# GpSimd layer norm in a fused cross-attention and FFN block: mean subtracted in the normalising instruction

## What is computed

```
def _layernorm(x, axis=-1, eps=1e-05):
    m = jnp.mean(x, axis=axis, keepdims=True)
    v = jnp.var(x, axis=axis, keepdims=True)
    return (x - m) / jnp.sqrt(v + eps)
...
    x = x + _L0_xattn_ref(_layernorm(x, axis=-1), ctx_1024, ctx_1024, mask_SxS2_bk1, ...)
    x = x + _L0_ffn_ref(_layernorm(x, axis=-1), L0_ffn_w1, L0_ffn_b1, L0_ffn_w2, L0_ffn_b2)
```

## Time and profile before

| | |
|---|---|
| median of 3 runs | 397.78 us (395.81 to 399.18) |
| the profiled execution | 397.82 us, its span 396.0 us |
| TensorE (PE) busy | 340.2 us, 86% of the span |
| VectorE (DVE) busy | 333.1 us, 84% |
| GpSimd (POOL) busy | 312.6 us, 79% |
| ScalarE (ACT) busy | 259.5 us, 66% |
| granted TensorE clock, mean | 0.954 |

### The profile page before, as it was taken

The page is one execution under the profiler, slowest core; times in us unless marked ns, Lnnn a source line. Parts: engine busy times, 40 slices in busy tenths (PEclk is TensorE's granted clock), DMA queues, the critical chain, the costliest instruction groups (busy, mean ns, idle before and its releaser), DMA issues. The chain is left out here.

```text
span 396.0 us, 7941 instructions
## 1 busy us (share of the span) xinstructions
PE 340.2 (86%) x2387; PEld 230.0 (58%) x2387; DVE 333.1 (84%) x722; ACT 259.5 (66%) x486; POOL 312.6 (79%) x460
## 2 busy tenths in 40 slices
PE   5888979999797997979888979798897988889793
PEld 3544645758474756656564747474655656465562
DVE  1978889999799897989898979889898989897555
ACT  1078276788685776776767668587676776768370
POOL 1304739769989899898898898989899899886856
PEclk9975569999999999999999999999999999999898
DMA  8800101010202011111102020201011111001012
GB/s 261 290 2 1 54 0 55 2 54 2 106 2 105 4 57 49 53 53 53 53 29 77 0 106 0 106 0 67 38 53 53 53 53 53 0 0 55 0 55 106
DMA packets 9424, 21.39 MB, mean 54 GB/s; under 512 B 1720, under 2 KB 4928, under 8 KB 9408
## 3 DMA queue, kind: packets, MB, share of 16 engines
q1 hardware_dynamic: 8496, 21.14, 14.8%
q10 hardware_dynamic: 912, 0.05, 0.2%
HBM read 12.80 MB, written 8.39 MB: 54 GB/s over the span
## 5 line engine op out<-in xcount | busy, mean ns | idle before, releaser
L649 DVE SCALAR_TENSOR_TENSOR h_lo<-h_sb,h_scale,h_hi 128x512 f16<-128x512 f32 x128 | 113.4, 915 | 11.2 <-POOL h_hi L419 7.0
L1234 PE MATMUL psZ<-sgn2T,h_hi 128*128 128x256 f16 x512 | 117.8, 275 | 0.5 <-DVE sgn2T L868 0.2
L1234 PE MATMUL psZ<-sgn2T,h_lo 128*128 128x256 f16 x512 | 117.5, 275 | 0.0
L498 ACT ACTIVATE h_sb<-psY,b_col,alpha1x 128x512 f32<-128x512 f32 x128 | 94.7, 777 | 8.5 <-PE psY L1220 5.9
L1220 PE MATMUL psY<-x_hi,sgn1T 128*128 128x512 f16 x256 | 97.6, 381 | 1.6 <-ACT sgn1T L621 1.6
L1220 PE MATMUL psY<-x_lo,sgn1T 128*128 128x512 f16 x256 | 97.5, 381 | 0.0
L419 POOL TENSOR_SCALAR h_hi<-h_sb,h_scale 128x512 f16<-128x512 f32 x64 | 48.2, 757 | 21.9 <-PE psZ L1234 19.7
L409 POOL TENSOR_SCALAR xh<-x,rstd,nmr 128x256 f32<-128x256 f32 x64 | 62.6, 990 | 3.4 <-issue 1.9
L1170 PE MATMUL psW<-ident,xh 128*128 128x128 f32 x256 | 36.4, 288 | 31.4 <-POOL xh L409 31.4
L1234 PEld LDWEIGHTS psZ<-sgn2T,h_hi 128*128 128x128 f16 x512 | 50.4, 98 | 13.9 <-DVE h_lo L649 5.2
L442 POOL TENSOR_TENSOR z_sb<-z_sb,x1b 128x256 f32<-128x256 f32 x62 | 56.5, 941 | 0.0
(11 more groups left out here) (151 smaller groups left out, 524.0 us busy)
## 6 DMA issues: line engine op xcount, KB each, us to landing
x_in<-in_x SPq DMA_DIRECT2D x16, 512.0 KB, 3.4
out_x<-z_sb SPq DMA_DIRECT2D x15, 512.0 KB, 2.6
w_sb<-in_L_ffn_w SPq DMA_DIRECT2D x2, 1024.0 KB, 9.5
ctx_sb<-in_ctx SPq DMA_DIRECT2D x1, 1024.0 KB, 6.7
out_x<-z_sb SPq DMA_DIRECT2D x2, 256.0 KB, 2.2
wk_sb<-in_L_xattn_Wk SPq DMA_DIRECT2D x1, 256.0 KB, 3.2
wq_sb<-in_L_xattn_Wq SPq DMA_DIRECT2D x1, 256.0 KB, 3.6
wv_sb<-in_L_xattn_Wv SPq DMA_DIRECT2D x1, 256.0 KB, 7.1
```

Source lines behind the costliest of these rows:

```text
L498: nc.scalar.activation(h_sb[c % 4][:, :], psY[c % 4][:, :], ACT.Gelu, bias=b1_col[:, c:c + 1], scale=alpha1x[:, c:c + 1]) \
L649: nc.vector.scalar_tensor_tensor(out=h_lo[c % 4][:, :], in0=h_sb[c % 4][:, :], scalar=h_scale[:, :], in1=h_hi[c % 4][:, :], op0=ALU.mult, ...
L1234: last = nc.tensor.matmul(psZ[j // 2][:, (j % 2) * D:(j % 2 + 1) * D], part[c % 4][:, j * P:(j + 1) * P], sgn2T[:, c, :], start=(c == 0 an ...
```

## The change

Two of the small steps of the norm, `nmean` and `nmr`, are no longer made, and their tiles are gone. The four instructions that write `xh` take the mean straight from `st` and `rstd`, and compute `(src - mean) * rstd`. `rstd` now waits for `vare` alone; `norm_steps` counts two steps for a norm where it counted four. Nothing else is touched.

```diff
--- before.py
+++ after.py
@@ -148,10 +148,8 @@
         x_in = [sb(f"x_in{n}", [P, T, D]) for n in range(2)]
         st_raw = [sb(f"st_raw{n}", [P, T, 6]) for n in range(2)]
         st = [sb(f"st{n}", [P, T, 2]) for n in range(2)]
-        nmean = [sb(f"nmean{n}", [P, T]) for n in range(2)]
         vare = [sb(f"vare{n}", [P, T]) for n in range(2)]
         rstd = [sb(f"rstd{n}", [P, T]) for n in range(2)]
-        nmr = [sb(f"nmr{n}", [P, T]) for n in range(2)]
         xh = [sb(f"xh{n}", [P, T, D]) for n in range(2)]
         xT_hi = sb("xT_hi", [P, KD, S], F16)
         xT_lo = sb("xT_lo", [P, KD, S], F16)
@@ -394,21 +392,16 @@
                 wait_apart(pool, stats[n], val(i, par, 1, 1))
                 nc.gpsimd.tensor_scalar(vare[n][:, :], st[n][:, :, 1], 1.0, EPS, ALU.mult, ALU.add) \
                     .then_inc(norm_steps[n], 1)
-                nc.gpsimd.tensor_scalar(nmean[n][:, :], st[n][:, :, 0], -1.0, 1.0, ALU.mult,
-                                        ALU.mult).then_inc(norm_steps[n], 1)
-                wait(pool, norm_steps[n], val(i, par, 4, 2))
+                wait(pool, norm_steps[n], val(i, par, 2, 1))
                 nc.gpsimd.tensor_tensor(rstd[n][:, :], vare[n][:, :], mhalf[:, :], ALU.pow) \
                     .then_inc(norm_steps[n], 1)
-                wait(pool, norm_steps[n], val(i, par, 4, 3))
-                nc.gpsimd.tensor_tensor(nmr[n][:, :], nmean[n][:, :], rstd[n][:, :], ALU.mult) \
-                    .then_inc(norm_steps[n], 1)
 
                 wait(pool, (x_turned, x1_turned)[n], val(i, par - 1, KD, KD))
-                wait_apart(pool, norm_steps[n], val(i, par, 4, 4))
+                wait_apart(pool, norm_steps[n], val(i, par, 2, 2))
                 for j in range(T):
                     last = nc.gpsimd.tensor_scalar(xh[n][:, j, :], src[:, j, :],
-                                                   rstd[n][:, j:j + 1], nmr[n][:, j:j + 1],
-                                                   ALU.mult, ALU.add)
+                                                   st[n][:, j, 0:1], rstd[n][:, j:j + 1],
+                                                   ALU.subtract, ALU.mult)
                 last.then_inc(normed[n], 1)
 
             def hi(i, par, c):
```

## The result

The changed kernel takes 452.7 us (median of 4 runs, 449.0 to 454.0) where the kernel before takes 397.7: a ratio of 1.137, 95% interval 1.129 to 1.145. It is slower, by 55 us. The forecast was 383.5 us with a range of 379 to 396.

The account below looks back on a forecast made before the run. A loop through GpSimd and both norms was taken to bound the kernel. Gains of 12.1 (steady window), 1.1, 0.55 and 0.57 summed to 14.3 us: 396.0 - 14.3 + 1.8 = 383.5 us, range 379 to 396.

Parts of the forecast that it names:

- The four legs: Loop closing a batch: GpSimd L395 to first transpose 4.85, to second 6.84, to fourth `h_hi` 2.24, to next L395 7.35 us.
- What is removed: `nmean` and `nmr` go in each norm: by spacing of starts 0.57 us a norm, 1.14 a batch.
- the other form of batch: Four of the window's 11 batches, second leg 7.06 us, batch 21.50; forecast to fall to 6.49 and 20.36, gaining 1.14.
- the time before 81.30: Start of the kernel, where GpSimd waits for others up to 13.8 us at a time; no gain counted.
- the batch from 81.30: Batch ahead of the steady window, its L395 waiting for VectorE; expected to give its two norms' 1.1 us.
- from 337.29 on: Tail behind the steady window: half of 1.1 us for two norms, plus 0.57 for the last second norm.
- What is changed: `xh` as (src - mean) * rstd on GpSimd, eight instructions a batch: price taken as unchanged, 0.55 us each.
- The end above: Upper bound for one `xh` instruction: 0.69 us, from a two-tensor add of the same size (L451).
- The argument from L419: GpSimd's multiply-multiply handles twice the elements for 0.13 us more, so multiply-add is not visibly favoured; supports an unchanged price.
- The one on the other side: Dearer subtraction in `xh`: 397 to 398 us at 0.69 each, 439 at twice the price; chance 0.19, 0.10 for slower.
- The collision rival: Moved second-norm `xh` blocked by three VectorE `h_lo`, 0.40 us a batch back: 388.5 us, or 392; chance 0.17.
- GpSimd isn't the master: VectorE or TensorE follow their own loops, only one norm's 0.57 us counts: 391 us, or less gain; chance 0.06.

Follow-up runs that it names:

- the cheap pair: The changed kernel with `xh` written by multiply, add instead of subtract, multiply on the same operands, so the norm is not computed; 378.45 us, ratio 0.951.
- the second list: The kernel before with 13 extra GpSimd instructions at the start, among them single operations and pairs with immediates, to read their prices; 398.4 us, one run.
- the run with the second norm slow: The kernel before with subtract, multiply on its own operands in the second norm only, so that norm is not computed; 437.42 us.

## Why the prediction was wrong

**What bounds the kernel: right.** The four legs through both norms hold in the changed kernel (6.79, 7.91, 2.25, 7.34 in nine batches of 11, give or take 0.2 us in all) and with the cheap pair (183.79 - 180.07 = 3.72, then 190.52 - 183.79 = 6.73, 2.25 and 7.34).

**What is removed: right.** 0.28 and 0.29 us a norm, as rows. (By lengths the steady part would give 12.5 - 8.9 = 3.6 us less, where the prediction says 3.7.) With the price unchanged the gain was 19.8 us, more than the 14.3 forecast. Of the sum, the terms missed were these: the steady part gave 11 x 1.31 = 14.4 instead of 12.1, by two errors of opposite sign: the first norm's `xh` came free of its collision (0.55 us a batch, which I had kept), and the second leg ended at GpSimd's 6.73 and not at 6.34 or, in the other form of batch, 6.49, 0.24 to 0.39 us a batch less gained; the time before 81.30 gave 2.5, counted as nothing (L393 of that batch is at 78.78); the batch from 81.30 gave 0, counted as 1.1; from 337.29 on it was 3.3, counted as 1.1.

**What is changed: the step that failed.** "The nearest row is the instruction itself with two other operators, so I take 0.55, no change." It measured 1.22. The end above, 0.69 from a two-tensor add, was no bound either: it was a row of another instruction, and it left the true price outside the range. The argument from L419 was the trap. Multiply-multiply was as cheap as multiply-add, and from two cheap pairs I concluded that the pair doesn't matter. The comparison was also uneven: L419 has one column and an immediate, and that form takes 0.48 us for 256 elements (L398 of the second list), so twice the elements cost 0.20 us more, not 0.13. They are two of the three cheap ones among the twelve pairs tried with two columns. A sentence earlier stood what should have weighed more: the trace has no subtract on this engine. Other instructions of the trace gave the price of this pair no bound from above, and with eight instructions a batch on the path it was the largest term of the sum.

The rule of the Trainium skill (GPSIMD Engine Reference, Elementwise), that a body with up to two operations is held by the ports at about 1.03 cycles an element, agrees roughly with the cheap pairs: 0.81 ns an element for mult/add, where the rule with the 1.2 GHz of the same page's Specifications makes an estimate of 0.86. The page gives the number of operations and names none; "whichever they are" was the prediction's reading, and it doesn't hold for subtract/mult at 3.34 ns. The measurement decides.

**The rivals.** The one on the other side had the right place and mechanism, the point from which it decides (0.14 us an instruction) and, at twice the price, 439 us. It got a chance of 0.10 for slower. At the measured 1.22 it would have read 8 x 0.67 - 1.14 = 4.2 us a batch. The batch shown lost 3.0, for there the slow `xh` are blocked less: the second norm's four lose 5.63 - 4 x 1.22 = 0.75 us to VectorE instead of 1.8, the first's 0.3 instead of 0.5. The mean is 3.2, because of the two batches in which TensorE came late, which no term of the prediction had. The collision rival was not what happened: with the cheap pair the second norm's four `xh` take 4.17 us, inside the 4.00 to 4.24 of before, and a batch 20.05. That GpSimd isn't the master is refuted: the time follows its instructions both up and down, and by more than one norm's share.

**What would make it wrong** was named first in its list: undisturbed `xh` over 0.6 us. The profile after shows it in one row.

## What to carry to other kernels

On GpSimd a `tensor_scalar` has a price for its pair of operators: multiply and add in the combinations mult/add, add/mult and mult/mult cost 0.55 us for 128 x 256 with two columns (0.41 with two immediates), everything else tried, single operations too, 0.86 to 1.24. Write an affine step with one of the three, turn a sign on the small operand beforehand, and add a second operator "multiply by 1.0" rather than leave it out. Before trusting an unchanged price for an operator that no row shows on that engine, put one such instruction into idle time and read its row: the loop was modelled to 0.2 us a batch here, in part by errors that cancelled, and the forecast fell on a factor of 2.2 in one instruction.

## What the runs showed of the hardware

- The price list above: 0.81 ns an element for three pairs, 3.34 for subtract/mult; (925 - 457)/192 = 2.44 for a single multiply (457 ns at 64 elements); 0.07 to 0.08 us for each column scalar.
- TensorE's clock fell to 0.50 (1.2 GHz) behind idle times of 3.97 and 2.67 us; behind 2.01 and 2.16 us, in the run with the second norm slow, the eight transposes took 1.09 us, as at full clock. The same idle time of 2.67 to 2.69 us before the second transposes left them at 1.09, 1.18, 1.70 and 1.97 us in four batches of that run, and behind 3.60 us in the changed kernel they took 1.09 us in one batch and 1.97 in another, so the fall doesn't come at a fixed point of the wait. It costs time where the next thing that waits for TensorE has no slack: 13.8 us in one kernel, about 2 us in the steady part of another with similar idle times (3.6 to 3.8 us). In the first, filling the wait with useless matmuls gave it back; in the other, collisions took most of it again.
- Where GpSimd and VectorE collide, either engine can be the one that pays. Before, the first norm's `xh` beside an `h_lo` lost 0.5 us and the `h_lo` nothing (0.72). With the cheap pair in the changed kernel the same `h_lo` met GpSimd's `h_hi` instead: the `h_lo` took 1.15, the `h_hi` 0.69 as when undisturbed, and GpSimd's 128 x 4 instruction behind it 0.51 instead of 0.20. Which one pays decides whether the batch gets longer, since only GpSimd was on the path.
